# Attention scores on TensorE: two 64x128 matmuls per chunk written as four 64x64 ones

## What is computed

```python
Q, K, V = x @ W_Q, x @ W_K, x @ W_V          # per tier: 4, 8 and 12 heads of 64
K = K + einsum('bthr,hrd->bthd', c_k, Pk)    # tiers 0 and 1; V likewise
scores = einsum('bhqd,bhkd->bhqk', Qh, Kh) / sqrt(64)
scores = where(causal, scores, -1e30)
out = einsum('bhqk,bhkd->bhqd', softmax(scores), Vh)
x = x + concat(out) @ W_O
x = x + layernorm(layernorm(x)) @ ternary(weight).T + bias
```

## Time and profile before

| what | us |
|---|---|
| median of 2 runs | 4717.3 (4699.7 and 4734.91) |
| the profiled execution | 4691.21 |
| its span on the slowest core (core 4) | 4689.7 |
| spans of the 8 cores | 4656.5 to 4689.7 |
| first and last score matmul (line 653) begin | 875.0 and 3677.5 |

### The profile page before, as it was taken

One profiled execution on the slowest core, in us unless ns is written; L12 is line 12 of the kernel. 1 busy time (PEld: TensorE's weight loads), 2 busy tenths in 40 slices (PEclk: granted clock), 3 DMA queues, 4 the chain that ended last, 5 costly groups with the idle time before them and its releaser, 6 DMA issues. The chain is left out here.

```text
span 4689.7 us, 32293 instructions; the slowest of 8 cores (4656.5 to 4689.7 us)
## 1 busy us (share of the span) xinstructions
PE 2564.8 (55%) x9732; PEld 868.6 (19%) x9732; DVE 1438.9 (31%) x2249; ACT 1549.3 (33%) x1340; POOL 199.7 (4%) x340
## 2 busy tenths in 40 slices
PE   2028003675757676767675867666775315600279
PEld 0013001221212121212121212222221002200134
DVE  3311320233333332333333333333333143145123
ACT  1424420143434444434343434434444300044000
POOL 2101110000000000000000000000000010000000
PEclk9999556787878787878686868788877657755689
DMA  4785765001010101010100000000000465422764
GB/s 106 196 198 173 210 176 121 19 3 30 3 28 3 30 3 30 3 30 3 29 3 27 5 15 17 11 22 11 17 6 4 94 196 183 156 93 99 141 160 135
DMA packets 285241, 326.96 MB, mean 70 GB/s; under 512 B 230291, under 2 KB 233363, under 8 KB 270739
## 3 DMA queue, kind: packets, MB, share of 16 engines
q1 hardware_dynamic: 241430, 185.68, 15.9%
q0 software_dynamic: 43648, 139.21, 9.6%
HBM read 203.99 MB, written 100.66 MB: 65 GB/s over the span
## 5 line engine op out<-in xcount | busy, mean ns | idle before, releaser
L737 ACT ACTIVATE psb<-s_ps,cshift,cone 128x1024 bf16<-128x1024 f32 x960 | 1149.1, 1204 | 986.4 <-PE s_ps L657 980.5
L589 PE MATMUL kvp<-lnxT,kwsb 128*128 128x512 bf16 x1536 | 434.7, 415 | 551.1 <-DMA vwsb<-d_veff 502.3
L673 PE MATMUL oA<-psb,vtb 128*65 128x512 bf16 x960 | 418.6, 436 | 187.9 <-DVE psb L836 148.6
L605 PE MATMUL kvp<-lnxT,vwsb 128*128 128x512 bf16 x1536 | 424.2, 406 | 13.6 <-DVE vfm L767 6.9
L653 PE MATMUL s_ps<-qsb,ksb 64*128 64x512 bf16 x960 | 414.8, 432 | 5.2 <-ACT bc_sb L744 4.7
L657 PE MATMUL s_ps<-qsb,ksb 64*128 64x512 bf16 x960 | 415.2, 433 | 0.0
L1195 PE MATMUL fps<-wqT,xnT 128*128 128x512 bf16 x1024 | 224.7, 383 | 338.7 <-DMA wqT<-d_wq 338.7
L677 PE MATMUL oB<-psb,vtb 128*65 128x512 bf16 x960 | 407.2, 424 | 0.0
L834 DVE TENSOR_TENSOR psb<-psb,masks_sb 128x512 bf16<-128x512 bf16 x384 | 163.2, 425 | 669.4 <-ACT psb L737 669.3
L589 PEld LDWEIGHTS kvp<-lnxT,kwsb 128*128 128x128 bf16 x1536 | 152.2, 104 | 806.6 <-issue 675.5
L431 PE MATMUL q_ps<-lnownT,wqsb 128*128 128x512 bf16 x528 | 130.1, 411 | 269.0 <-DMA lnownT<-d_lnown 226.2
(11 more groups left out here) (145 smaller groups left out, 2173.1 us busy)
## 6 DMA issues: line engine op xcount, KB each, us to landing
xtF<-x_full SPq DMA_DIRECT2D x32, 1024.0 KB, 6.8
d_lnx<-lsF POOLq DMA_DIRECT2D x32, 512.0 KB, 7.3
wfa<-wffn SPq DMA_DIRECT2D x32, 512.0 KB, 4.4
wfq<-wffn POOLq DMA_DIRECT2D x16, 1024.0 KB, 7.9
xot<-x_own SPq DMA_DIRECT2D x16, 1024.0 KB, 6.6
d_x<-x1s POOLq DMA_DIRECT2D x16, 1024.0 KB, 8.6
x1t<-d_x SPq DMA_DIRECT2D x16, 1024.0 KB, 4.8
x1h<-d_x SPq DMA_DIRECT2D x32, 512.0 KB, 4.8
```

The lines of the kernel that those rows point to most:

```text
L589: last = t.matmul(kvp[:], kwsb[:, 128 * fc:128 * (fc + 1)], lnxT[:, T * fc + 512 * gq:T * fc + 512 * (gq + 1)], start=(fc == 0), stop=(fc ...
L605: last = t.matmul(kvp[:], vwsb[:, 128 * fc:128 * (fc + 1)], lnxT[:, T * fc + 512 * gq:T * fc + 512 * (gq + 1)], start=(fc == 0), stop=(fc ...
L673: t.matmul(oAp[0:65, :], vtb[pr % 2][:, 130 * c:130 * c + 65], psb[sl][:, 0:512], start=(c == 0), stop=(c == nch - 1))
L737: _inc(a.activation(psb[sl][:], s_ps[:, 1024 * sl:1024 * (sl + 1)], AF.Exp, bias=cshift[:], scale=cone[:]), aE, 1)
```

## The change

The two matmuls of `emit_scores` become four. The 128 columns of weights, which are the 128 keys of the chunk, are cut into two halves of 64, and each head's product is made half by half: keys 0 to 63 go to PSUM partitions 0 to 63, keys 64 to 127 to partitions 64 to 127. `tile_position` names for each the 64x64 quarter of the array in which it runs. The order is head A low half (0, 0), head B high half (64, 64), head A high half (0, 64), head B low half (64, 0). The banks, the data, the waits and the one count of `tS` (now on the fourth) stay. Each of the four streams 512 columns.

```diff
-                t.matmul(s_ps[:, 1024 * sl:1024 * sl + 512],
-                         ksb[pr % 2][0:64, 128 * c:128 * (c + 1)],
-                         qsb[0:64, 512 * j:512 * (j + 1)],
-                         start=True, stop=True)
-                _inc(t.matmul(s_ps[:, 1024 * sl + 512:1024 * sl + 1024],
-                              ksb[pr % 2][64:128, 128 * c:128 * (c + 1)],
-                              qsb[64:128, 512 * j:512 * (j + 1)],
-                              start=True, stop=True), tS, 1)
+                cA = 1024 * sl
+                cB = 1024 * sl + 512
+                qA = qsb[0:64, 512 * j:512 * (j + 1)]
+                qB = qsb[64:128, 512 * j:512 * (j + 1)]
+                t.matmul(s_ps[0:64, cA:cA + 512],
+                         ksb[pr % 2][0:64, 128 * c:128 * c + 64], qA,
+                         start=True, stop=True, tile_position=(0, 0))
+                t.matmul(s_ps[64:128, cB:cB + 512],
+                         ksb[pr % 2][64:128, 128 * c + 64:128 * c + 128], qB,
+                         start=True, stop=True, tile_position=(64, 64))
+                t.matmul(s_ps[64:128, cA:cA + 512],
+                         ksb[pr % 2][0:64, 128 * c + 64:128 * c + 128], qA,
+                         start=True, stop=True, tile_position=(0, 64))
+                _inc(t.matmul(s_ps[0:64, cB:cB + 512],
+                              ksb[pr % 2][64:128, 128 * c:128 * c + 64], qB,
+                              start=True, stop=True, tile_position=(64, 0)), tS, 1)
```

## The result

The changed kernel takes 4725.1 us in the median of 43 runs, the kernel before 4706.1 in that of 42. The ratio is 1.0043, with a 95% interval of 1.0027 to 1.0059, so the change costs 13 to 28 us, 20 at its middle. The forecast was +33 us, too little for a measurement that tells 2% apart. The direction holds and the change is within 2%; the size is a little over half of the forecast.

What follows compares the result with a forecast made beforehand. TensorE was taken to bound most of the attention. 614 chunks x 1.2 for the clock x 0.045 us (18 + 27 ns) gave 33 us, from 4699.7 to 4733 us, +0.7%; range 4690 to 4885.

Steps and rivals of the forecast that it cites:

- What bounds the kernel: Through most of the attention the other engines wait for TensorE; a longer score step lengthens an unmasked 1.74 us chunk.
- The narrower load, 18 ns: Score step: the first pair of 64-column loads costs the path 26 ns, 18 more than the 128-column loads.
- The second pair of loads, 27 ns: Score step: loads (0, 64) and (64, 0), in the same array rows as the first pair, cost about 27 ns more.
- d: What the score step gets longer in one chunk; forecast 0.045 us.
- The end at 0.018: Score step: second loads go fully beside the first, d = 0.018 us; +13 us, 4713.
- How often d counts: Attention: 614 chunks, times 1.2 for the low clock; hidden at unmasked group starts, half per chunk in masked loops.
- Loads paid whole: Rival, score step: second loads wait and are paid whole, d = 0.126 us; 93 us, 4793; chance 0.14.
- column halves one after the other: Rival, score step of every chunk: column halves stream in turn, d = 0.234 us; 172 us, 4872; chance 0.20.
- All four one after the other: Rival, score step: the four matmuls run in turn, d = 0.666 us; about 558 us, 5258; chance 0.05.
- The clock's return: Rival, transposing chunks and those after: four matmuls keep TensorE's clock up, 4593; chance 0.05 together with a shorter exit.

Runs made afterwards that it cites:

- 96 columns: Kernel before with 96 instead of 128 weight columns in each of its two score matmuls, last 32 keys of each chunk left out; attention 23.2 us longer.
- two narrow matmuls: Changed kernel with only the score matmuls (0, 0) and (64, 0), half of each chunk's keys left out; attention 15.5 us longer than in the kernel before.
- eight tiles: Kernel before with the same scores in eight 64x32 matmuls in place of two 64x128; attention 30.4 us longer.
- the pair issued twice: Kernel before with its two score matmuls issued twice in every chunk, a known price of one slot, 0.216 us; ratio 1.0354.
- both orders: The change's order and changed kernel reordered (0,0), (0,64), (64,0), (64,64); attention 18.4 and 21.7 us longer than in the kernel before.

## Why the prediction was right, and where its size was off

*What bounds the kernel.* Right. Unmasked chunks in which nothing hid the score step became longer by 17 to 18 ns in the medians of position by position (cores 4 to 7, pairs 1 to 10). Unmasked chunks that begin a new group, 1.97 us, changed by no more than 1. The masked loop of two chunks grew by 28. The waits agree but are weak evidence: from 1000 to 3600 us ScalarE waits 929.2 us for the scores, against 925.9, in a stretch of fixed length that now holds fewer chunks.

```profile
ACT psb L745 <- PE s_ps L666: 929.2, 737, 19.8
```

*The narrower load, 18 ns.* Measured 13, with the sign that few would expect: less is loaded and it takes longer. I had read it off the modelled lengths of the 65-column row; the starts of oA with 32, 64 and 96 columns (0, 13 and 27 ns later) order themselves by width. The Trainium skill (TensorEngine Tiling (Array Packing), Restrictions) states that column tiling disables Fast Weight Load. The 13 ns of the changed kernel don't contradict it. But the run with 96 columns and no column tile loses the same way, so the width alone is enough; and the row that the prediction took as bearing the statement out, of 65 columns, was no column tile either, so it showed the width and not the tiling.

*The second pair of loads, 27 ns.* This is the term that was mis-sized. It was taken from oB's load, 0.03 behind oA's, which goes into the same columns. The second pair goes into columns of its own, and the runs show 7 ns for it, all of it the later start of the last matmul. So d = 0.020, not 0.045, and in the prediction's sum 614 x 1.2 x 0.020 = 15 us. The end at 0.018, which the prediction gave as the case of loads side by side, was nearer. The entry to the scores, at which the prediction did not look for a change, gave 3 ns back (309 against 312); the same 309 stand in the runs of 32, 64 and 96 columns, and 311 to 312 in the two that begin with a 128-column load. Why is not known.

*What the sum left out.* The prediction said that ScalarE and VectorE would see exactly d. They see more: the exponential starts 30 ns later, TensorE goes on 20 ns later. In the masked loops (about 170 of them) this adds 170 x 0.008 = 1.4 us. Of the eight transposing chunks of a pair four are masked and four are not. The masked ones, at the lower clock, grew by 46 ns, where oA is 31 later and the exponential 45: they too go through the exponential. In the other runs their growth follows it as well, 26 ns for 28 with two narrow matmuls, 53 for 55 with 96 columns, 52 for 52 with eight tiles. They add 44 x 0.016 = 0.7 us. The unmasked ones grew by 29 to 33, with oA. Together 17 us against the measured 20 (13 to 28); what is left is within the interval.

*How often d counts.* Borne out by the pair issued twice, 1.0354 against 1.034, and by the group starts that didn't move.

*The rivals.* Loads paid whole and column halves one after the other: refuted by starts within 0.01 us in both orders, with oA at 0.34. All four one after the other: likewise. The clock's return: 0.21 of the score matmuls at 1.2 GHz on core 4, as before, so no.

*Time.* 4733 was forecast, 4725 measured; part of the closeness is luck. The prediction stood on 4699.7, where the kernel before measured 4706.1, and from that base 33 us would have given 4739. The base was 6 us too low and the change was put 13 us too high.

## What to carry to other kernels

Splitting a matmul that already shares the array by rows into column tiles buys nothing: the same columns stream in the same slot, and loads of 64 columns cost 13 ns more than those of 128 where nothing hides them. Eight tiles of 32 columns avoid this but hand over the result still later. Look in the timeline for neighbours whose starts are a full duration apart while they use only a few rows of the array; giving these rows of their own took 1.6% off this kernel with two changed lines. Keep neighbours in one shape: each change of shape in these traces took 0.31 to 0.34 us from start to start where a stream takes 0.216.

## What the runs showed of the hardware that was not expected

- A load of 96 columns lasts 116 ns, of 64 columns 103, of 32 columns 89, and of 128 columns 93. All but the last grow with the width. The starts say the same: oA begins 347, 333, 340 and 320 ns after the first score matmul, and of the 340 with 32 columns 20 are the later start of the eighth matmul.
- More column tiles delay the result more than the engine: with two matmuls of 64 columns the exponential starts 562 ns after the first score matmul, with four 578, with eight of 32 columns 598 (548 before the change), while oA starts at 333, 340 and 340. Whether the shared rows, the shared PSUM bank or the number of matmuls does it was not tested.
- A 64x128 matmul and a 64x64 one in other rows don't run together (0.31 us apart), while four 64x64 do (0.01).
- fp32 matmuls of one row, in two recorded passes each, interleave when their rows differ: the first passes last 1.19 and 1.22 us and start 0.01 apart, the second passes last 1.06 and start 0.04 apart. In the same row they follow one another.
